# The two running maxima of a graph attention kernel move from PSUM to SBUF

## Chip, cores, metric

One core of one Trainium2 chip. The metric is the time of one launch on the device in microseconds (us); lower is better.

## The reference, cut to what matters

```python
h = jnp.maximum(_layernorm(x), 0.0)                # x: 3125 nodes x 128
x = x + gat(relu(gat(h, W1 ...)), W2 ...)          # two layers, 103125 edges (src, dst)
h = jnp.maximum(_layernorm(x), 0.0)
x = x + gat(h, W ...)                              # third layer

def gat(x, src, dst, W, a_src, a_dst, b):
    h = x @ W
    e = leaky_relu((h @ a_src)[src] + (h @ a_dst)[dst], 0.2)
    m = segment_max(e, dst)
    ex = exp(e - m[dst])
    z = segment_sum(ex, dst)
    return segment_sum((ex / z[dst])[:, None] * h[src], dst) + b
```

The attention is a softmax over the edges that end in a node. For it the kernel needs, for each destination node, the greatest source term among its neighbours.

## The kernel before

The 3125 nodes are 25 tiles (T) of 125 (P). The kernel does not walk the edges in the layers. It first builds a matrix C of edge counts, source by destination, held whole in SBUF as 8-bit floats: 125 partitions (sources within a tile) by 5 chunks (NC) by 25 source tiles by 625 destinations (CD). A count is stored as half of itself.

**Count stage** (to about 204 us). VectorE (DVE) compares keys with an iota (`one_hots`, line 951), 40 steps (NT); TensorE multiplies the one-hot matrices (`count`, line 1780) and signals `half_ok`; ScalarE writes the result into C (line 1452) and signals `half_out`. The one-hots lie in `scratch`, in two buffers by the parity of the step. The first chunk of the first layer is already multiplied by POOL and TensorE in this stage, but not its maxima.

**Layers.** 15 chunks (Q = 3 layers x 5), each 625 destinations by 25 source tiles `s`. For each tile:
- a product block of 125 x 625 in a ring of `slot`s: either DVE makes it (`product`, line 1149: maximum of the row term in PSUM and a scalar, times C), or ScalarE does the maximum in two passes (lines 1567 and 1569) and POOL (GpSimd) multiplies by C (line 751). In a chunk of the last layer POOL has 15 of the 25 tiles; it also scales and adds the chunk before (lines 756, 767, 776, 779).
- TensorE multiplies the block with the features (`products`, line 1813, and `last_products`, line 1821), into PSUM banks 0 and 1.

**The running maxima.** Beside that DVE finds the greatest source term of each destination, chunk by chunk. `top_step` (lines 1051 to 1069) takes the minimum of the counts and a scalar of the source tile (0 where there is no edge, the scaled term where there is) and the maximum with what is there: one instruction of 625 elements for each of the 25 tiles. There are two running maxima, for even and for odd tiles (`in_odd`), so that two instructions that follow each other do not wait for each other's result; the first of each is a tensor_scalar (line 1069), the others scalar_tensor_tensor (line 1067). The last odd one is written to `top_a`, in SBUF, and `join_tops` (line 1073) joins the even maximum into it. TensorE transposes `top_a` (line 1789), DVE reduces it (line 1079), and from that come the factors `back`, `kappa` (ScalarE, line 1550) and `rz` for the softmax of the chunk. The maxima of a chunk run while the products of the same chunk run, 5 of them (AHEAD) at the end of the chunk before; in the first layer they are spread by `FIRST_TOPS`, since none was made in the count stage.

**Where things lie.** In the usual path both running maxima lie in PSUM at columns TOP0 and TOP1. `side` and `side_c` are two blocks of 625 columns of `scratch` in SBUF, at columns 4405 and 5030, which only the careful path (a branch that these inputs do not take) used; they lie over the one-hot buffer of the odd steps (columns 4096 to 8191).

**Order.** Every engine runs its list in the order written. Before the first maximum DVE makes the last one-hots (step 39, an odd one, lines 1248 and 1249) and waits for `half_out[1]` (line 1250), that is for the ScalarE copy of step 38. `set_mode`, `extremes_early`, `negative_r` (line 1040) and others are small instructions on DVE between the large ones; line 880 is one of the start.

Of the kernel before, what the change touches and what calls it, by code (L numbers as in the profile page):

```python
# [7 lines left out]
def gat_stack_kernel(nc, x, edges, apart, W1, a_src1, a_dst1, b1, W2, a_src2, a_dst2, b2,  # L8
# [3 lines left out]
    ALU, ACT, AX = mybir.AluOpType, mybir.ActivationFunctionType, mybir.AxisListType  # L12
# [6 lines left out]
    P = 125  # L19
# [16 lines left out]
    CD = CT * P  # L36
# [17 lines left out]
    NT = NC * JT  # L54
# [12 lines left out]
    with ctx:  # L67
# [3 lines left out]
        def sem(name):  # L71
            return ctx.enter_context(nc.semaphore(name))
# [113 lines left out]
        top_a = scratch[0:P, at:at + CD]  # L186
# [13 lines left out]
        side = scratch[0:P, at:at + CD]  # L200
        side_c = scratch[0:P, at + CD:at + 2 * CD]
# [4 lines left out]
        ps = ctx.enter_context(nc.psum_tensor("ps", [128, 8 * 512], fp32))  # L206
# [12 lines left out]
        ROWU, TOP1, TOP0, WORK, NEW = 1024, 1664, 2304, 3072, 3072  # L219
# [58 lines left out]
        half_ok = [sem("half0_ok"), sem("half1_ok")]  # L278
# [164 lines left out]
        def in_odd(k, q=None):  # L443
            if q in (1, 2):
                return k % 2 == 1 and not any(at_ == AFTER and (c, k) == (q, k_) for at_, c, k_ in FIRST_TOPS[q])
            return k >= AHEAD and k % 2 == 1
# [423 lines left out]
        def _(dve):  # L870
            v = nc.vector
# [68 lines left out]
            def one_hots(t, part=None):  # L940
                c, i = t // JT, t % 2
                first, last_w = SPLIT[t % JT], SPLIT[t % JT + 1]
                w0, w1_ = 0, last_w - first
                if part is not None:
                    w0, w1_ = HALF[part][0], min(HALF[part][1], w1_)
                if t > 1 and w0 == 0:
                    dve.wait_ge(half_ok[1], t - 1)
                for n, (hot, key, m) in enumerate(((hot_lo[i], key_lo, COLS), (hot_col[i], key_col, P))):
                    if t % JT == 0:
                        dve.wait_ge(keys_sb, 2 * c + n + 1)  # L950
                    last = v.tensor_tensor(hot[:, w0:w1_, :, :],  # L951
                                           key[:, c, first + w0:first + w1_, :].unsqueeze(2).broadcast_to(
                                               [128, w1_ - w0, m, LANES]),
                                           iota_ps[:, 0:m, :].unsqueeze(1).broadcast_to([128, w1_ - w0, m, LANES]),
                                           ALU.is_equal)
                last.then_inc(hots_ok, 1)
# [94 lines left out]
            def top_step(S, unit, q, s):  # L1051

                counts = C5[:, q % NC, s, :]
                n = q * (T + 1)
                odd = in_odd(s, q if S is F else None)
                at_ = TOP1 if odd else TOP0
                top = ps[0:P, at_:at_ + CD]
                same = [k for k in range(s) if in_odd(k, q if S is F else None) == odd]
                if same:
                    dve.wait_ge(S.top_done, n + same[-1] + 1)  # L1060
                elif q:
                    dve.wait_ge(S.top_done, n)
                if s == LAST_ODD and q:
                    dve.wait_ge(S.top_T, q)
                dest = top_a if s == LAST_ODD else top
                if same:
                    v.scalar_tensor_tensor(dest, counts, unit[:, s:s + 1], top, ALU.min, ALU.max).then_inc(S.top_done, 1)  # L1067
                else:
                    v.tensor_scalar(dest, counts, unit[:, s:s + 1], None, ALU.min).then_inc(S.top_done, 1)  # L1069

            def join_tops(S, q):
                dve.wait_ge(S.top_done, q * (T + 1) + T)
                v.tensor_tensor(top_a, top_a, ps[0:P, TOP0:TOP0 + CD], ALU.max).then_inc(S.top_done, 1)

            def maxima(S, q, part, scale, low):
                tc = slice(q % NC * CT, (q % NC + 1) * CT)
# [76 lines left out]
            def next_top(q, k):  # L1153
                L = q // NC
                if turn(q) and k in (0, EARLY_TILES, LATE):
                    dve.wait_ge(unit_ready, 3 * L - 1 + (0, EARLY_TILES, LATE).index(k))
                top_step(F, a_unit[L % 2], q, k)

            def first_tops(q, s):
                for at_, c, k in FIRST_TOPS[q]:  # L1160
                    if at_ == s:
                        next_top(c, k)
                        if k == T - 1:
                            join_tops(F, c)

            def chunk(q):
                L, c = q // NC, q % NC
                for s in range(T):
# [4 lines left out]
                    if q < len(FIRST_TOPS):  # L1173
                        first_tops(q, s)
                    else:
                        for k in range(AHEAD, T):
                            if top_at(q, k) == s:
                                next_top(q, k)
                        if s == join_at(q):
                            join_tops(F, q)  # L1180
# [67 lines left out]
            one_hots(NT - 1, 0)  # L1248
            one_hots(NT - 1, 1)
            dve.wait_ge(half_out[1], NT)  # L1250
            dve.wait_ge(unit_ready, 1)
            for k in range(AHEAD):
                next_top(0, k)
# [113 lines left out]
            def careful_chunk(q):  # L1367
                L, c = q // NC, q % NC
                b = ab[L][:, c * CT:(c + 1) * CT, 1]
                for i in range(T):  # L1370
                    top_step(K, a_unit[0], q, i)
                join_tops(K, q)
                for part in range(3):
                    maxima(K, q, part, span[:, 1:2], b_low[0])
                if q:
                    dve.wait_ge(K.rows_ready, q)
                dve.wait_ge(K.m_lin, 2 * q + 2)
                v.tensor_tensor(uv[:, 0, :], b, m_top[:, :], ALU.subtract)
                v.scalar_tensor_tensor(uv[:, 1, :], b, SLOPE, m_top[:, :], ALU.mult, ALU.subtract).then_inc(uv_ready, 1)
                for s in range(T):  # L1380
                    A, B, n = slot[s], side, q * T + s
                    dve.wait_ge(e_ready, n + 1)
                    v.tensor_tensor(B, A, B, ALU.max).then_inc(mx_done, 1)
                    dve.wait_ge(mx_done, n + 1)
                    v.scalar_tensor_tensor(A, B, 2.0, C5[:, c, s, :], ALU.min, ALU.mult).then_inc(p_ready, 1)
                    if c:
                        careful_after(q - 1, s)
                    if s == LEAD - 1:
                        rest_steps(q)
# [308 lines left out]
        def _(pe):  # L1698
# [71 lines left out]
            def count(t, by_halves=False):  # L1770
                i, n = t % 2, SPLIT[t % JT + 1] - SPLIT[t % JT]
                for j, (w0, w1_, _) in enumerate(HALF):
                    at_ = place(t, j)
                    if j == 0 or by_halves:
                        pe.wait_ge(hots_ok, t + 1 + j)
                    pe.wait_ge(half_out[j], t + 1)
                    for w in range(w0, min(w1_, n)):
                        o = at_ + 128 * (w - w0)
                        for k in range(KC):
                            last = mm(ps[0:128, o:o + WC], hot_lo[i][:, w, :, k], hot_col[i][:, w, :, k],  # L1780
                                      start=(k == 0), stop=(k == KC - 1))
                    last.then_inc(half_ok[j], 1)
# [260 lines left out]
```

## Time and profile before

| what | us |
|---|---|
| median of 3 runs | 687.71 (687.67 to 689.26) |
| the profiled execution | 687.7 |
| its span, first to last instruction | 686.0 |
| busy in the span: DVE | 639.8 (93%) |
| PE (TensorE) | 587.9 (86%) |
| ACT (ScalarE) | 484.7 (71%) |
| POOL (GpSimd) | 459.6 (67%) |

The profiled execution lies at the median of the runs. The profile is of this one execution. Start times count from the start of the span. PEld is TensorE's weight load beside the matmuls. A group of instructions is named by its line, engine, operation and "out<-in" by the program's names; `ps` is the PSUM tensor, `C`, `scratch`, `gathered`, `hB` and the rest lie in SBUF.

### The profile page before, as it was taken

What the parts mean: (1) busy time and instruction counts of PE and PEld (TensorE: products, weight loads), DVE (VectorE), ACT (ScalarE), POOL (GpSimd) and SP (SyncE); (2) the same over time, 40 slices, a digit from 0 to 9 for tenths busy, and PEclk for the clock granted to TensorE, in tenths of its full rate; (3) what the DMA queues carried; (4) which work ended last, traced back from release to release, by engine and by line L of the source; (5) the groups of instructions that cost most, each with busy time, mean ns of one, the idle gap of its engine ahead of it and who ended that gap; (6) DMA issues with size and microseconds to landing.
All of it is one profiled execution on the core that took longest, in us unless ns stands there. A gap on an engine that the chain in (4) does not pass through costs nothing.

```text
span 686.0 us, 13824 instructions
## 1 busy us (share of the span) xinstructions
PE 587.9 (86%) x5571; PEld 570.1 (83%) x5571; DVE 639.8 (93%) x911; ACT 484.7 (71%) x719; POOL 459.6 (67%) x448
## 2 busy tenths in 40 slices
PE   1728845989869899999999979999989989999995
PEld 1628744988769899989999979899989979999994
DVE  3999979999999989999987999999998899999994
ACT  0416543655969787887765878989886698898891
POOL 5579103589908656675954775858598688697883
PEclk9959977899999899999999999999999999999998
DMA  2410002000000000000100100000010010110001
GB/s 69 119 56 2 1 9 38 1 2 1 20 1 1 20 1 20 1 1 9 20 20 1 27 1 20 1 19 2 8 20 20 1 27 3 37 29 11 20 1 42
DMA packets 22325, 12.07 MB, mean 18 GB/s; under 512 B 12393, under 2 KB 20055, under 8 KB 22255
## 3 DMA queue, kind: packets, MB, share of 16 engines
q1 hardware_dynamic: 21455, 9.85, 6.2%
q0 software_dynamic: 800, 1.26, 0.6%
q8 instruction: 46, 0.75, 0.5%
q14 instruction: 24, 0.20, 0.1%
HBM read 9.47 MB, written 1.64 MB: 16 GB/s over the span
## 4 chain that ended last, share of the span: by engine, by line
DVE 52%; PE 28%; issue 8%; DMA 6%; POOL 4%; ACT 1%; POOLq 0%; DVEq 0%; SPq 0%
PE ps L1813 21%; DVE scratch L951 21%; DVE ps L1067 16%; DVE scratch L1149 5%; DMA xr<-in_x 3%; POOL scratch L751 2%; DVE ps L1069 2%; DVE ps L1079 1%; PE ps L1866 1%; PE ps L1821 1%; DMA gathered<-ext_lines 1%; PE ps L1844 1%; DVE scratch L1067 1%; DMA gathered<-in_edges,start_i 1%; DMA ext_lines<-ext 1%
## 5 line engine op out<-in xcount | busy, mean ns | idle before, releaser
L1813 PE MATMUL ps<-hB,scratch 125*125 125x129 f32 x3450 | 404.7, 276 | 21.3 <-DVE scratch L1149 17.8
L1813 PEld LDWEIGHTS ps<-hB,scratch 125*125 125x125 f32 x3450 | 390.7, 189 | 28.6 <-DVE scratch L1149 23.0
L751 POOL TENSOR_TENSOR scratch<-scratch,C 125x625 f32<-125x625 f32 x239 | 304.1, 1283 | 124.1 <-ACT scratch L1569 122.1
L1067 DVE SCALAR_TENSOR_TENSOR ps<-C,a_unit,ps 125x625 f32<-125x625 fp8e3 x330 | 275.5, 867 | 2.3
L1567 ACT ACTIVATE scratch<-gathered,r_neg 125x625 f32<-125x625 f32 x219 | 176.6, 806 | 18.7 <-PE ps L1813 17.5
L1569 ACT ACTIVATE scratch<-scratch,r_src 125x625 f32<-125x625 f32 x219 | 179.0, 817 | 7.1
L1452 ACT ACTIVATE C<-ps 125x1000 fp8e3<-125x1000 f32 x80 | 78.0, 1000 | 78.5 <-PE ps L1780 78.3
L1780 PE MATMUL ps<-scratch 128*128 128x125 bf16 x1250 | 90.3, 235 | 40.0 <-DVE scratch L951 38.1
L1780 PEld LDWEIGHTS ps<-scratch 128*128 128x128 bf16 x1250 | 83.0, 105 | 46.8 <-DVE scratch L951 44.7
L1149 DVE SCALAR_TENSOR_TENSOR scratch<-ps,r_src,C 125x625 f32<-125x625 f32 x121 | 104.2, 861 | 4.2 <-PE ps L1803 4.1
L951 DVE TENSOR_TENSOR scratch<-key_lo,ps 128x4096 bf16<-128x4096 bf16 (+3 forms) x41 | 89.8, 2190 | 0.0
L951 DVE TENSOR_TENSOR scratch<-key_col,ps 128x4000 bf16<-128x4000 bf16 (+3 forms) x41 | 87.9, 2144 | 0.0
L1069 DVE TENSOR_SCALAR ps<-C,a_unit 125x625 f32<-125x625 fp8e3 x30 | 25.8, 865 | 0.2
L756 POOL TENSOR_TENSOR scratch<-scratch,rz 125x640 f32<-125x640 f32 x14 | 17.6, 1258 | 11.8 <-DVE rz L1126 11.8
L743 POOL TENSOR_SCALAR scratch<-gathered,r_src 125x625 f32<-125x625 f32 x20 | 15.7, 783 | 10.7 <-DMA gathered<-g_lines 10.7
L1550 ACT ACTIVATE kappa<-back 125x5 f32<-125x5 f32 x15 | 3.1, 207 | 27.0 <-DVE back L1093 26.9
L1821 PE MATMUL ps<-hB,scratch 125*125 125x129 f32 x150 | 21.6, 274 | 0.0
L1821 PE MATMUL ps<-hB,gathered 125*125 125x129 f32 x150 | 21.4, 273 | 0.0
L728 POOL TENSOR_TENSOR shift<-sigma,tau 125x1 f32<-125x1 f32 x3 | 0.6, 192 | 30.7 <-DVE tau L1013 30.7
L1079 DVE TENSOR_REDUCE ps<-ps 125x5 f32<-125x625 f32 x15 | 12.2, 812 | 8.2 <-PE ps L1789 8.2
L790 POOL TENSOR_TENSOR hB<-hA,e_src 125x645 f32<-125x645 f32 x15 | 19.0, 1265 | 0.0
L1821 PEld LDWEIGHTS ps<-hB,scratch 125*125 125x125 f32 x150 | 18.8, 187 | 0.2 <-POOL scratch L751 0.2
(195 smaller groups left out, 451.5 us busy)
## 6 DMA issues: line engine op xcount, KB each, us to landing
gathered<-g_lines SPq DMA_DIRECT2D x15, 305.2 KB
xr<-in_x SPq DMA_DIRECT2D x1, 1562.5 KB
out<-xr SPq DMA_DIRECT2D x4, 312.5 KB
edge_sb<-in_edges SPq DMA_DIRECT2D x1, 805.7 KB
gathered<-ext_lines SPq DMA_DIRECT2D x5, 122.1 KB
w<-in_W SPq DMA_DIRECT2D x2, 128.0 KB
out<-xr SPq DMA_DIRECT2D x1, 187.5 KB
out<-xr SPq DMA_DIRECT2D x1, 125.0 KB
```

The lines of the kernel that those rows point to most:

```text
L751: g.tensor_tensor(slot[s], slot[s], C5[:, q % NC, s, :], ALU.mult).then_inc(pool_done, 1)
L951: last = v.tensor_tensor(hot[:, w0:w1_, :, :], key[:, c, first + w0:first + w1_, :].unsqueeze(2).broadcast_to([128, w1_ - w0, m, LANES]), ...
L1067: v.scalar_tensor_tensor(dest, counts, unit[:, s:s + 1], top, ALU.min, ALU.max).then_inc(S.top_done, 1)
L1069: v.tensor_scalar(dest, counts, unit[:, s:s + 1], None, ALU.min).then_inc(S.top_done, 1)
L1079: v.tensor_reduce(mu[:, :], tiles(WORK), AX.X, ALU.max).then_inc(S.top_max, 1)
L1149: v.scalar_tensor_tensor(slot[s].rearrange("p (t n) -> p t n", n=P), tiles(ROWU), r_src[L % 2][:, s:s + 1], C5[:, c, s, :].rearrange("p (t ...
L1452: a_.activation(C5[:, c, :, rows].rearrange("p t (w q) -> p t w q", q=WQ), tiles(place(t, i), w1_ - w0).rearrange("p w (t q) -> p t w q", ...
L1567: a_.activation(A, ga[q % 2], ACT.Relu, bias=r_neg[L % 2][:, s:s + 1]).then_inc(over_done, 1)
L1569: a_.activation(A, A, ACT.Identity, bias=r_src[L % 2][:, s:s + 1]).then_inc(rowmax_ok, 1)
L1780: last = mm(ps[0:128, o:o + WC], hot_lo[i][:, w, :, k], hot_col[i][:, w, :, k], start=(k == 0), stop=(k == KC - 1))
L1813: last = mm(ps[0:P, acc_at(t):acc_at(t) + HW], A[:, P * t:P * (t + 1)], feat, start=opens and t in (0, 3), stop=closes, skip_group_check=True)
L1821: last = mm(ps[0:P, acc_at(t):acc_at(t) + HW], slot[s][:, P * t:P * (t + 1)], hB3[:, s, :], start=False, stop=s == T - 1, skip_group_check ...
```

## The change

Both running maxima of the usual path take the two blocks `side` and `side_c` of `scratch`, in SBUF, in place of the two in PSUM; `top_a` stays where it was. All maxima and the join read and write there. Since the blocks lie over the odd one-hot buffer, DVE also waits, before the first maximum, until TensorE has multiplied the last step (`half_ok[1]`). `top_step` and `join_tops` are shared with the careful path, whose maxima move too.

```diff
@@ top_step
                 odd = in_odd(s, q if S is F else None)
-                at_ = TOP1 if odd else TOP0
-                top = ps[0:P, at_:at_ + CD]
+                top = side if odd else side_c
@@ join_tops
-                v.tensor_tensor(top_a, top_a, ps[0:P, TOP0:TOP0 + CD], ALU.max).then_inc(S.top_done, 1)
+                v.tensor_tensor(top_a, top_a, side_c, ALU.max).then_inc(S.top_done, 1)
@@ before the first maximum
             dve.wait_ge(half_out[1], NT)
+            dve.wait_ge(half_ok[1], NT)
             dve.wait_ge(unit_ready, 1)
```

## Rows read from the trace of the kernel before

**Rows 1.** Stretches: busy time (instructions) of each engine, granted PE clock, DMA.

```profile
core 0: us, PE busy (x) PEld busy (x) DVE busy (x) ACT busy (x) POOL busy (x), PEclk, DMA share, GB/s
0.00:203.29 203.29, 137.25 (x1616) 128.03 (x1616) 187.29 (x168) 102.00 (x138) 115.56 (x122) 0.91 0.11 27
203.29:671.00 467.71, 444.12 (x3902) 436.04 (x3903) 447.62 (x726) 381.73 (x579) 340.27 (x324) 0.99 0.05 13
671.00:686.00 15.00, 6.51 (x56) 6.04 (x54) 4.88 (x19) 0.97 (x3) 3.77 (x3) 0.88 0.17 45
```

**Rows 2.** Stretches: one chunk of the last layer.

```profile
203.29:224.20 20.91, 18.51 (x165) 17.87 (x165) 20.71 (x27) 20.37 (x27) 15.53 (x16) 1.00 0.01 2
594.82:623.98 29.16, 28.97 (x260) 28.77 (x260) 28.95 (x45) 25.67 (x36) 23.87 (x20) 1.00 0.08 23
```

**Rows 3.** Page, part 4: the chain that ended last, by engine.

```profile
DVE 52%; PE 28%; issue 8%; DMA 6%; POOL 4%; ACT 1%; POOLq 0%; DVEq 0%; SPq 0%
```

**Rows 4.** Groups on DVE: busy us, mean ns, idle before.

```profile
L1067 DVE SCALAR_TENSOR_TENSOR ps<-C,a_unit,ps 125x625 f32<-125x625 fp8e3 x330 | 275.5, 867 | 2.3
L1149 DVE SCALAR_TENSOR_TENSOR scratch<-ps,r_src,C 125x625 f32<-125x625 f32 x121 | 104.2, 861 | 4.2 <-PE ps L1803 4.1
...
L1069 DVE TENSOR_SCALAR ps<-C,a_unit 125x625 f32<-125x625 fp8e3 x30 | 25.8, 865 | 0.2
L1067 DVE SCALAR_TENSOR_TENSOR scratch<-C,a_unit,ps 125x625 f32<-125x625 fp8e3 x15 | 12.9, 859 | 0.0
...
L1073 DVE TENSOR_TENSOR scratch<-scratch,ps 125x625 f32<-125x625 f32 x15 | 12.1, 808 | 0.5
```

**Rows 5.** Groups on POOL, 203 to 671 us: the products.

```profile
L751 POOL TENSOR_TENSOR scratch<-scratch,C 125x625 f32<-125x625 f32 x207 | 262.8, 1281 | 113.0 <-ACT scratch L1569 112.6
```

**Rows 6.** Timeline: start us, duration us, what. POOL and DVE together.

```profile
605.71 3.68 POOL L751 TENSOR_TENSOR scratch<-scratch,C 125x625 f32<-125x625 f32 x3
...
606.24 3.19 DVE L1067 SCALAR_TENSOR_TENSOR ps<-C,a_unit,ps 125x625 f32<-125x625 fp8e3 x4
```

**Rows 7.** Timeline at 393 us.

```profile
393.44 1.25 POOL L751 TENSOR_TENSOR scratch<-scratch,C 125x625 f32<-125x625 f32 x1 [0.31 <-ACT scratch L1569]
393.49 1.20 DVE L1020 SCALAR_TENSOR_TENSOR counts_fit<-ext_all,covers 1x1 f32<-1x1 f32 x1
```

**Rows 8.** Groups on DVE: small instructions.

```profile
L1086 DVE SCALAR_TENSOR_TENSOR ps<-ps,e_top 125x5 f32<-125x5 f32 x15 | 2.5, 165 | 0.0
...
L1113 DVE TENSOR_TENSOR ps<-scratch,kappa x14: 152/166/170, 229.5 to 657.2; 125x5 f32<-125x5 f32 x14
```

**Rows 9.** Timeline at 359 us.

```profile
359.44 1.26 POOL L756 TENSOR_TENSOR scratch<-scratch,rz 125x640 f32<-125x640 f32 x1
360.00 0.73 DVE L1040 TENSOR_SCALAR r_neg<-r_src 125x5 f32<-125x5 f32 x1
```

**Rows 10.** Timeline at 3 us.

```profile
3.11 1.53 POOL L636 IOTA hB<- 128x256 bf16 x1
3.27 1.71 DVE L880 TENSOR_SCALAR scratch<-hA,sampled 125x625 f32<-125x625 f32 x1 [0.52 <-POOL numbers L634]
```

**Rows 11.** Timeline at 15 us.

```profile
14.54 1.21 POOL L641 DMA_INDIRECT gathered<-in_edges,start_i  x1 [0.30 <-issue]
...
16.02 0.28 DVE L913 TENSOR_SCALAR hB<-hB 125x256 f32<-125x256 f32 x1
16.05 1.33 POOL L641 DMA_INDIRECT gathered<-in_edges,start_i  x1 [0.30 <-issue]
```

**Rows 12.** Groups on DVE: two inputs in SBUF, in the tail.

```profile
L1244 DVE SCALAR_TENSOR_TENSOR xr<-scratch,rz,xr 125x128 f32<-125x128 f32 x5 | 1.5, 348 | 0.1
```

**Rows 13.** Timeline of POOL at 591 us; in brackets the idle time before.

```profile
591.65 1.25 POOL L751 TENSOR_TENSOR scratch<-scratch,C 125x625 f32<-125x625 f32 x1 [2.68 <-ACT scratch L1569]
```

**Rows 14.** Timeline at the end of the count stage.

```profile
203.29 0.90 DVE L1069 TENSOR_SCALAR ps<-C,a_unit 125x625 f32<-125x625 fp8e3 x1
...
203.47 0.76 PE L1780 MATMUL ps<-scratch 128*128 128x125 bf16 x10 [0.33 <-DVE scratch L951]
```

**Rows 15.** Stretches of the count stage.

```profile
86.00:103.00 17.00, 8.29 (x98) 7.53 (x96) 13.54 (x18) 7.99 (x15) 1.25 (x5) 0.80 0.05 9
137.00:154.00 17.00, 14.73 (x186) 14.00 (x184) 17.00 (x9) 9.39 (x12) 13.85 (x13) 1.00 0.01 2
```

## Prediction

> **What bounds the kernel now.** I read the stretches first. Until 203.29 us the kernel counts edges and no running maximum exists; from there to 671.00 the attention layers run, and the last 15.00 us are the tail [rows 1]. Only the middle stretch, 467.71 us, holds instructions that the change touches. In it VectorE (DVE) is busy 447.62 us, TensorE 444.12, ScalarE 381.73 and GpSimd (POOL) 340.27: two engines are at 95%, ScalarE is at 82% and POOL at 73%. One chunk of the last layer (29.16 us) shows the same more sharply: PE 28.97, DVE 28.95, POOL 23.87, ACT 25.67 [rows 2]. The chain that ended last puts 52% on DVE and 28% on PE [rows 3]. So time that DVE loses between two products goes nearly whole into the end, and POOL can lose about 5 us a chunk before it sets the pace itself.
>
> Then the groups. The running maxima of the usual path are 330 scalar_tensor_tensor of 867 ns, which read the counts in SBUF and the maximum in PSUM, and 30 tensor_scalar of 865; 15 more of the first kind write top_a, and 15 joins take 808 [rows 4]. That is 390 instructions, 26 a chunk. DVE's other large work, the products (121 into scratch, 10 into the last slot), reads its rows from PSUM and stays as it is. POOL's work is 207 products of 1281 ns in that stretch, each reading two tensors in SBUF [rows 5]. Last, what the two engines do at once: four maxima follow each other in 3.19 us, so (3.19 - 0.86)/3 = 0.777 us from start to start, while POOL has three products of its own in 3.68 us, 1.21 apart [rows 6]. Neither feels the other. Today no running maximum takes two tensors from SBUF.
>
> **What the change does.** It removes and adds no instruction but one wait. All 360 maxima and joins get two SBUF inputs, and the 30 tensor_scalar have SBUF on both sides. The question is what such an instruction costs beside a busy POOL, and the trace has it in small samples:
> - At 393.49 a scalar_tensor_tensor of one element, both tensors in SBUF, took 1.20 us and ended at 394.69; a POOL product ran from 393.44 to 394.69 [rows 7]. Its kind, with one input in PSUM, takes 165 ns [rows 8]. So it waited about 1.04 us, until some 0.16 before the recorded end of POOL's instruction.
> - At 360.00 a tensor_scalar of 5 elements, SBUF to SBUF, took 0.73 and ended at 360.73; POOL's instruction ended at 360.70 [rows 9].
> - At 3.27 a tensor_scalar of 625 elements took 1.71 and ended at 4.98; a POOL iota ended at 4.64 [rows 10]. It ran within 0.34 + 0.16 = 0.50 us once let in.
> - Against it: the 14 small products with kappa have two SBUF inputs too and took 152 to 170 ns [rows 8]. Each started where POOL had no large instruction under way, since they stand behind the exponential for which ScalarE and then POOL wait; so they don't contradict it.
>
> I read: such a DVE instruction is let in only when the POOL instruction under way is through. The Trainium skill ("SBUF — State Buffer", section "Who interferes with whom") says that a DVE instruction with two SBUF inputs contends with a GpSimd instruction that reads SBUF, that a 2-port mode does too, and that whichever starts first keeps the shared pair for the whole instruction. By that rule the sum is the serial one below; the trace agrees for DVE waiting on POOL (1.20 us for one element).
>
> The other direction, POOL waiting for DVE, has one weak sample: the POOL instruction at 16.05, beside a DVE tensor_scalar from SBUF to SBUF at 16.02, took 1.33 where the one before took 1.21 [rows 11]. I take it as mutual.
>
> **The sum.** If the two exclude each other, the stretch must hold all of POOL's instructions and all 390 maxima one after the other; products of DVE (131) and its small work still lie beside POOL.
> - Upper end: POOL 340.3 us as it is, maxima 390 x 0.777 = 303.0. Together 643.3.
> - Lower end: POOL lets go 0.16 us early in each of its 324 instructions [rows 1], 340.3 - 51.8 = 288.5. DVE holds only while it streams: from 128 elements in 348 ns [rows 12] and 625 in 861 [rows 4], (861 - 348) / 497 = 1.032 ns an element and 216 ns fixed, so it streams 0.645 us; 360 x 0.645 = 232.2. The tensor_scalar's 0.50 less the same 0.22 is 0.28, 30 x 0.28 = 8.4. Together 529.1.
> - I take the middle, 586: handing over hides something of each instruction's fixed part, but not all in an engine that issues in order.
> - Idle port: once a chunk POOL has nothing ready for about 2.7 us (a wait for ScalarE at 591.65) [rows 13]. 14 x 2.7 = 37 us. At most maxima fill it (nothing added); I keep it, since the products of DVE come late now and free the buffers late. Stretch: 623 us.
>
> The added wait: DVE's first maximum starts at 203.29, and the last count matmuls, whose buffers the new place overlaps, end at 203.47 + 0.76 = 204.23 [rows 14]. Queued behind it are all maxima and products of chunk 1; DVE is 20.7 of 20.9 us busy there, so I take the whole 0.9 us; the lower bound is 0, if chunk 1 is paced by the port anyway.
>
> Sum against the profiled execution (span 686.0, run 687.7, so 1.7 outside; it equals the median of 687.71): 203.3 + 0.9 + 623 + 15.0 + 1.7 = 844 us. Ends of the same case: 529 + 37 gives 787, 643 + 37 gives 901. One chunk as a cross-check: 23.9 + 26 x 0.777 = 44.1, at the lower end 20 x (1.21 - 0.16) + 24 x 0.645 + 2 x 0.28 = 37.0, middle 40.6 and 2.7 idle, 43 us in place of 29.2.
>
> What is late next: POOL's products reach PE later, so PE, now waiting 0.2 us in such a chunk, falls to 444 of 623 us busy (71%).
>
> **The rivals.**
> *Only DVE waits.* POOL starts its next instruction although a DVE maximum is reading. Then a maximum beside a busy POOL costs 1.21 in place of 0.777, 0.43 more, for each POOL product that meets one: 207 x 0.43 = 89 us at most, 67 if a quarter fall on products instead. Stretch 535 to 557, end 756 to 778, say 770. For it: a sample for mutual exclusion hardly exists. Against: the instruction at 16.05 took 0.12 longer beside DVE, and POOL often waits for ScalarE between its products (113.0 us in all) [rows 5], so it is not always ready with the next one.
>
> *The clock falls.* With TensorE at 71%, its granted clock may drop to the lower level at times. From 137 to 154 us PE was busy 14.7 of 17 us at a granted clock of 1.00; from 86 to 103 it was busy 8.3 of 17 at 0.80, that is partly at 1.2 GHz in place of 2.4 [rows 15]. 71% lies between. At 0.80 the 444 us become 555: they fit into 623, but the chunks in which the fall hits stretch; half of the 111 us give 900 and more, up to 950 with the upper end of the sum.
>
> *Faster.* The samples above are special and the large forms stream past POOL. Then what stays is a cheaper maximum: a tensor_scalar from SBUF to SBUF needed 0.50 us when let in [rows 10] instead of 0.865, so 30 x 0.37 = 11 us of DVE. For the two-input forms I have drawn one line through 348 ns (both inputs in SBUF) and 861 (one in PSUM) [rows 4, 12]; were the true slope 1.0 ns an element, the fixed parts would be 220 and 236 ns, and at 0.95 it would be 226 and 267, so SBUF could save 0 to 40 ns, at most 14 us over 360. DVE is 52% of the chain: half of 11 to 25 us, 0.9 for the wait given back, 676 to 683 us. This rival holds if POOL's instructions release the port element by element rather than whole; the one-element instruction that took 1.20 us speaks against it. The Trainium skill ("VectorE: DVE Perf Modes", section "The TRN2 errata — SBUF-src ops pay a fixed extra latency per instruction") gives 58 cycles fixed from SBUF and 120 from PSUM. By its figures each of the 390 would save 62 cycles, 65 ns, an estimate of 25 us in all and about 676 us with half of it in the chain; no run so far shows it.
>
> *Nothing changes:* maxima fall into POOL's gaps. POOL is busy 340 of 468 us, so its gaps of 128 us cannot hold 303 us of maxima.
>
> **How the numbers follow.** Mutual exclusion 0.72, 844 (787 to 901). Only DVE waits 0.11, 770. Clock or the upper end passed 0.08, 900 to 950. Faster 0.06, 680. Same 0.03. About 0.3% is what a measurement can tell here. The range must hold 8 in 10: the first case with the greater part of the second, 765 to 905. Faster 0.06, same 0.03, slower 0.91.
>
> **What the profile after would show.** Right: maxima of 625 elements that take up to 1.9 us, their ends 0.5 to 0.7 us behind the end of a POOL product; POOL products with means well above 1281 ns, or spaced by 1.7 to 2.0 us; DVE's busy time up by far more than its instruction count; products from PSUM still at 861 ns; PE waiting for POOL and DVE in every chunk. POOL products still at 1.28 us and 1.21 apart beside long maxima: only DVE waits. A granted clock below 0.95 in the stretch: the second rival. Wrong altogether: maxima at 800 to 870 ns beside a busy POOL. The forecast fails in size first of all by the hold of one maximum and by how often the port lies idle.

## The result and the profile after

The changed kernel takes 852.04 us (median of 5 runs, 848.06 to 852.68), the kernel before 687.71; the ratio is 1.2367 (95% interval 1.2332 to 1.2401). The profiled execution of after is one of its shorter ones: 848.1 us, span 846.3. So it stands 160 us above the profiled execution before, and the median 164 us above the median.

The page's busy times, then the stretches (us, then busy time and instructions of PE, PEld, DVE, ACT, POOL, the granted clock, DMA): the layers and the tail, and one chunk of the last layer.

```profile
PE 641.7 (76%) x5571; PEld 614.7 (73%) x5571; DVE 803.2 (95%) x911; ACT 488.4 (58%) x719; POOL 588.2 (69%) x448
...
core 0: us, PE busy (x) PEld busy (x) DVE busy (x) ACT busy (x) POOL busy (x), PEclk, DMA share, GB/s
203.20:831.30 628.10, 495.93 (x3920) 478.73 (x3920) 608.30 (x724) 385.38 (x579) 468.84 (x324) 0.92 0.04 10
831.30:846.30 15.00, 4.62 (x38) 4.04 (x36) 7.57 (x21) 0.97 (x3) 3.81 (x3) 0.81 0.11 31
...
790.10:832.20 42.10, 33.55 (x257) 32.00 (x256) 41.85 (x46) 22.66 (x31) 34.13 (x20) 0.92 0.04 9
```

The layers take 628.1 us in place of 467.7, the tail the same 15.0 [rows 1]. ScalarE's busy time has hardly moved (385 and 382). DVE's has grown by 161 us and POOL's by 129, though neither has an instruction more. The chunk takes 42.1 in place of 29.2 us [rows 2], and DVE still counts as busy in 41.9 of them.

The groups (busy us, mean ns of one, idle before) say in which instructions the time lies:

```profile
L1066 DVE SCALAR_TENSOR_TENSOR scratch<-C,a_unit,scratch 125x625 f32<-125x625 fp8e3 x345 | 435.4, 1292 | 2.3
L1148 DVE SCALAR_TENSOR_TENSOR scratch<-ps,r_src,C 125x625 f32<-125x625 f32 x121 | 103.7, 857 | 4.5 <-PE ps L1803 4.5
...
L1068 DVE TENSOR_SCALAR scratch<-C,a_unit 125x625 f32<-125x625 fp8e3 x30 | 27.6, 924 | 1.1 <-issue 0.9
L1072 DVE TENSOR_TENSOR scratch<-scratch 125x625 f32<-125x625 f32 x15 | 22.9, 1526 | 0.5
...
L751 POOL TENSOR_TENSOR scratch<-scratch,C 125x625 f32<-125x625 f32 x239 | 386.2, 1632 | 142.3 <-ACT scratch L1569 140.3
L756 POOL TENSOR_TENSOR scratch<-scratch,rz 125x640 f32<-125x640 f32 x14 | 24.9, 1777 | 24.3 <-DVE rz L1125 24.3
...
L805 POOL TENSOR_TENSOR xr<-xr,b2r 125x128 f32<-125x128 f32 x25 | 21.3, 858 | 0.0
```

The 345 maxima took 867 ns in PSUM [rows 4] and take 1292 now, the joins 1526 in place of 808. DVE's product, which reads PSUM, is where it was (857 and 861). POOL's products went from 1.28 to 1.63 us over the whole run [rows 5 has those of the layers], although their own operands did not move. The excess on DVE is 345 x 0.426 + 15 x 0.718 + 30 x 0.059 = 147.0 + 10.8 + 1.8 = 159.6 us: all of the 160 by which the profiled execution is longer. Counted record by record, 227 of the 390 took over 0.95 us. Of the other 163 the two-input ones took about what they took before; the short tensor_scalars are looked at below.

One such meeting, in the timeline of DVE and of POOL:

```profile
807.27 1.83 DVE L1066 SCALAR_TENSOR_TENSOR scratch<-C,a_unit,scratch 125x625 f32<-125x625 fp8e3 x1
...
806.55 1.88 POOL L751 TENSOR_TENSOR scratch<-scratch,C 125x625 f32<-125x625 f32 x1 [1.32 <-ACT scratch L1569]
```

POOL's product ends at 806.55 + 1.88 = 808.43, the maximum at 809.10, 0.67 later. Over all two-input instructions among these 227 the end lies 0.665 to 0.670 us behind a POOL end (10th to 90th percentile, from the records). A maximum of 0.85 us is thus let in some 0.18 us before the recorded end of POOL's instruction, an estimate from the two lengths. The other direction is in the records too: 167 of POOL's 244 products took over 1.4 us, and the end of such a one lies 1.10 to 1.17 us behind the end of a maximum.

The tensor_scalar that begins each running maximum has only one input in SBUF, but its output is there as well. It waits in the same way:

```profile
575.36 1.61 DVE L1068 TENSOR_SCALAR scratch<-C,a_unit 125x625 f32<-125x625 fp8e3 x1
...
575.33 1.30 POOL L751 TENSOR_TENSOR scratch<-scratch,C 125x625 f32<-125x625 f32 x1 [4.62 <-ACT scratch L1569]
```

Its end is 0.34 us behind POOL's, and 21 of the 30 end 0.34 to 0.35 us behind one. Without a wait it takes about 0.54 us, so its mean of 924 ns hides both a gain and a wait.

And where both have work without a break:

```profile
820.62 0.86 DVE L1148 SCALAR_TENSOR_TENSOR scratch<-ps,r_src,C 125x625 f32<-125x625 f32 x1
821.40 6.84 DVE L1066 SCALAR_TENSOR_TENSOR scratch<-C,a_unit,scratch 125x625 f32<-125x625 fp8e3 x4
...
820.00 5.51 POOL L751 TENSOR_TENSOR scratch<-scratch,C 125x625 f32<-125x625 f32 x3
825.47 2.11 POOL L779 TENSOR_TENSOR xr<-xr,b3r 125x640 f32<-125x640 f32 x1
827.54 1.86 POOL L751 TENSOR_TENSOR scratch<-scratch,C 125x625 f32<-125x625 f32 x1
```

POOL starts a product at 820.00 and, three later, the next instruction at 825.47: 1.82 apart, and 1.82 again to 829.36. Before it was 1.21 [rows 6]. One maximum of DVE goes between two of POOL's. They take turns.

PE waited for DVE's products and for POOL's, and POOL for ScalarE (us in total, times, longest). The last line is from the kernel before:

```profile
POOL scratch L751 <- ACT scratch L1569: 140.3, 58, 17.6
...
PE ps L1813 <- DVE scratch L1148: 90.7, 56, 5.0
...
PE ps L1813 <- POOL scratch L751: 19.1, 12, 3.6
...
PE ps L1813 <- DVE scratch L1149: 17.8, 24, 3.6
```

### The profile page after: what moved, and what is told of

It is laid out like the page before. It is cut to its first block, busy times and chain, and to the rows that moved or that the text cites. A ratio compares the mean times of both kernels' runs of the same rounds, so it can differ in the third digit from the quotient of the medians.

```text
span 846.3 us, 13824 instructions
## 1 busy us (share of the span) xinstructions
PE 641.7 (76%) x5571; PEld 614.7 (73%) x5571; DVE 803.2 (95%) x911; ACT 488.4 (58%) x719; POOL 588.2 (69%) x448
## 4 chain that ended last, share of the span: by engine, by line
DVE 49%; issue 15%; POOL 6%; PE 5%; ACT 0%; POOLq 0%; DVEq 0%
DVE scratch L1066 34%; DVE scratch L1148 6%; PE ps L1813 4%; POOL scratch L751 3%; DVE scratch L1068 2%; DVE ps L1078 1%; DVE gathered L1148 1%; PE ps L1789 1%; DVE scratch L1072 1%; DVE bn6c L1132 0%; DVE scratch L951 0%; POOL hB L790 0%; POOL scratch L756 0%; POOLq L67 0%; DVE ps L1085 0%
## 5 line engine op out<-in xcount | busy, mean ns | idle before, releaser
L1813 PE MATMUL ps<-hB,scratch 125*125 125x129 f32 x3450 | 444.9, 290 | 110.0 <-DVE scratch L1148 90.7
L1813 PEld LDWEIGHTS ps<-hB,scratch 125*125 125x125 f32 x3450 | 424.7, 201 | 124.9 <-DVE scratch L1148 102.5
L751 POOL TENSOR_TENSOR scratch<-scratch,C 125x625 f32<-125x625 f32 x239 | 386.2, 1632 | 142.3 <-ACT scratch L1569 140.3
L1066 DVE SCALAR_TENSOR_TENSOR scratch<-C,a_unit,scratch 125x625 f32<-125x625 fp8e3 x345 | 435.4, 1292 | 2.3
L756 POOL TENSOR_TENSOR scratch<-scratch,rz 125x640 f32<-125x640 f32 x14 | 24.9, 1777 | 24.3 <-DVE rz L1125 24.3
L1068 DVE TENSOR_SCALAR scratch<-C,a_unit 125x625 f32<-125x625 fp8e3 x30 | 27.6, 924 | 1.1 <-issue 0.9
L1542 ACT ACTIVATE scratch<-ps 125x387 f32<-125x387 f32 x15 | 7.3, 490 | 34.3 <-PE ps L1821 34.3
L1821 PE MATMUL ps<-hB,scratch 125*125 125x129 f32 x150 | 23.1, 287 | 1.1 <-POOL scratch L751 0.6
L1072 DVE TENSOR_TENSOR scratch<-scratch 125x625 f32<-125x625 f32 x15 | 22.9, 1526 | 0.5
L790 POOL TENSOR_TENSOR hB<-hA,e_src 125x645 f32<-125x645 f32 x15 | 23.3, 1550 | 0.0
L1789 PE MATMUL ps<-ident,scratch 125*125 125x125 f32 x75 | 14.1, 332 | 12.0 <-DVE scratch L1072 11.3
```

Source lines behind the costliest of these rows:

```text
L751: g.tensor_tensor(slot[s], slot[s], C5[:, q % NC, s, :], ALU.mult).then_inc(pool_done, 1)
L1072: v.tensor_tensor(top_a, top_a, side_c, ALU.max).then_inc(S.top_done, 1)
L1813: last = mm(ps[0:P, acc_at(t):acc_at(t) + HW], A[:, P * t:P * (t + 1)], feat, start=opens and t in (0, 3), stop=closes, skip_group_check=True)
L1821: last = mm(ps[0:P, acc_at(t):acc_at(t) + HW], slot[s][:, P * t:P * (t + 1)], hB3[:, s, :], start=False, stop=s == T - 1, skip_group_check ...
```

## Experiments

### Which operand does it: reading or writing

The maximum can be put half in each memory. In the first kernel each reads the old maximum from PSUM and writes to SBUF; in the second it reads it from SBUF and writes to PSUM. The wait of the change is in both. The first edit is against the kernel before, the second against the kernel after; lines without a sign stand in both. The running maximum isn't carried on in either, so their attention is shifted by other values than the reference's.

```diff
 # reads PSUM, writes SBUF (against the kernel before)
                 top = ps[0:P, at_:at_ + CD]
+                to = side if odd else side_c
...
-                dest = top_a if s == LAST_ODD else top
+                dest = top_a if s == LAST_ODD else to if same else top
...
             dve.wait_ge(half_out[1], NT)
+            dve.wait_ge(half_ok[1], NT)
 # reads SBUF, writes PSUM (against the kernel after)
                 top = side if odd else side_c
+                at_ = TOP1 if odd else TOP0
+                to = ps[0:P, at_:at_ + CD]
...
-                dest = top_a if s == LAST_ODD else top
+                dest = top_a if s == LAST_ODD else to if same else top
```

> The 345 scalar_tensor_tensor read the counts from SBUF and the running maximum from PSUM, as before, but write to SBUF, as after. (The maximum is then not carried on: each takes the first of its set in place of the last. The first of each set and the join are as before.) If the second SBUF input is the cause: as before, 688 us (683 to 693), each 0.87 us, POOL products 1.28 us. If writing to SBUF, or SBUF as a place, is the cause: near 852 us.

Measured: 690.11 us, ratio 1.0021 (1.0012 to 1.0030). Maxima and POOL products (groups):

```profile
L1068 DVE SCALAR_TENSOR_TENSOR scratch<-C,a_unit,ps 125x625 f32<-125x625 fp8e3 x345 | 284.9, 857 | 2.4 <-POOL a_unit L718 0.2
...
L751 POOL TENSOR_TENSOR scratch<-scratch,C 125x625 f32<-125x625 f32 x239 | 304.7, 1288 | 124.7 <-ACT scratch L1571 122.6
```

> The 345 scalar_tensor_tensor read counts and running maximum from SBUF, as after, but write to PSUM, as before. (The maximum is not carried on; the first of each set goes to SBUF as after.) If the second SBUF input is the cause: as after, 852 us (842 to 858), means of 1.25 to 1.3 us, POOL products at about 1.8 us beside them. If it is the write: near 688 us.

Measured: 852.58 us, ratio 1.2375 (1.2356 to 1.2394).

```profile
L1068 DVE SCALAR_TENSOR_TENSOR ps<-C,a_unit,scratch 125x625 f32<-125x625 fp8e3 x330 | 421.9, 1308 | 2.3
...
L751 POOL TENSOR_TENSOR scratch<-scratch,C 125x625 f32<-125x625 f32 x239 | 387.0, 1636 | 144.3 <-ACT scratch L1571 142.0
```

For the scalar_tensor_tensor the write is free (690.1 is also what the added wait alone gives, below). The whole slowdown comes back with the second input in SBUF and the result in PSUM. It is the read, and it takes POOL's products along: 1288 ns without, 1636 with it. The two kernels say nothing of the 30 tensor_scalars, which write to PSUM in the first and to SBUF in the second.

### Is it POOL, or SBUF as a place

POOL's large instructions in the layers are cut to 5 columns, in the kernel after and in the kernel before. This leaves out most products, the scaling, the residual and the bias sums; every wait and signal stays. Of the edit only the product is shown, the others are of the same kind.

```diff
-                g.tensor_tensor(slot[s], slot[s], C5[:, q % NC, s, :], ALU.mult).then_inc(pool_done, 1)
+                n_ = CD if q == 0 else CT
+                g.tensor_tensor(slot[s][:, 0:n_], slot[s][:, 0:n_], C5[:, q % NC, s, 0:n_], ALU.mult).then_inc(pool_done, 1)
```

> The kernel after, with POOL's large instructions of the layer stretch cut to 5 columns (products, scaling, residual, biases; so most of that arithmetic is left out), all waits and signals kept. DVE's own work is untouched. Exclusion theory: with POOL's instructions at 0.2 us in place of 1.3 the maxima wait for next to nothing; a few us below the same cut of the kernel before, since the 30 tensor_scalar to SBUF save 0.3 us each: 672 to 692 us, maxima at 0.84 to 0.9 us. If SBUF is dearer by itself: over 50 us above that cut of the kernel before.

> The kernel before with the same cut of POOL's instructions. POOL had 5 us a chunk to spare in the last layer, so little changes: 675 to 688 us. It is the reference for the kernel after with the same cut: the difference of the two is what the place alone costs or gives, without POOL. Exclusion theory: within 10 us of each other, after not slower by more than 5.

Measured: 682.79 us after (ratio to the kernel before 0.9927, 0.9905 to 0.9950) and 683.01 before (0.9919, 0.9900 to 0.9938), so the 164 us between the two kernels are gone. First the groups of the cut kernel after, then of the cut kernel before:

```profile
L1068 DVE SCALAR_TENSOR_TENSOR scratch<-C,a_unit,scratch 125x625 f32<-125x625 fp8e3 x345 | 286.6, 862 | 2.3
...
L1070 DVE TENSOR_SCALAR scratch<-C,a_unit 125x625 f32<-125x625 fp8e3 x30 | 16.0, 536 | 1.6 <-issue 1.4
L1074 DVE TENSOR_TENSOR scratch<-scratch 125x625 f32<-125x625 f32 x15 | 12.3, 821 | 0.5
...
L752 POOL TENSOR_TENSOR scratch<-scratch,C 125x5 f32<-125x5 f32 x215 | 104.7, 491 | 277.3 <-ACT scratch L1571 277.0
```

```profile
L1069 DVE SCALAR_TENSOR_TENSOR ps<-C,a_unit,ps 125x625 f32<-125x625 fp8e3 x330 | 275.2, 865 | 2.3
...
L1071 DVE TENSOR_SCALAR ps<-C,a_unit 125x625 f32<-125x625 fp8e3 x30 | 25.8, 862 | 0.2
...
L752 POOL TENSOR_TENSOR scratch<-scratch,C 125x5 f32<-125x5 f32 x215 | 41.8, 196 | 362.3 <-ACT scratch L1571 361.0 <-PE ps L1815 1.4
```

Two things are to be read. Without POOL in the way a maximum costs the same from either memory, 862 and 865 ns; only the 30 tensor_scalar gain, 536 in place of 862 ns. And the other direction, which my prediction had from one weak sample, is plain here: POOL's instruction of 5 columns takes 196 ns on average beside maxima in PSUM and 491 beside maxima in SBUF. POOL waits for DVE too. The gain of the tensor_scalar, 30 x 0.33 = 9.8 us of DVE less 0.9 for the wait, doesn't show in the end.

### Half of the maxima

```diff
-                top = side if odd else side_c
+                top = ps[0:P, TOP1:TOP1 + CD] if odd else side_c
```

> Only the even running maximum lies in SBUF, the odd one is back in PSUM. Of the 26 instructions of a chunk 16 then have two inputs in SBUF (14 scalar_tensor_tensor, the join) or SBUF on both sides (one tensor_scalar), 10 have one input in PSUM. Exclusion theory: the port no longer sets the pace (POOL 288 to 340 us and 240 x 0.645 to 0.777 = 155 to 186 us are 443 to 526 us, against 448 us of DVE's own work), what is left are single waits of DVE; 240 instructions, 7 in 10 meeting a POOL instruction with half a microsecond to go, give 84 us: 740 to 780 us. If SBUF is dearer for each instruction by itself, the extra 164 us are shared by count: 16/26 of them, 789 us. Odd maxima stay at 0.87 us with both.

Measured: 788.79 us, ratio 1.146 (1.1442 to 1.1477). My 740 to 780 was too low, and the figure of the theory that a maximum in SBUF is dearer by itself, 789, was met. That theory is refuted by the kernels with short POOL instructions above (862 and 865 ns), so the meeting is by its count and not by its cause. The groups, and the border of two chunks in the timeline:

```profile
L1066 DVE SCALAR_TENSOR_TENSOR scratch<-C,a_unit,scratch 125x625 f32<-125x625 fp8e3 x210 | 263.3, 1254 | 2.3
...
L1066 DVE SCALAR_TENSOR_TENSOR ps<-C,a_unit,ps 125x625 f32<-125x625 fp8e3 x120 | 103.2, 860 | 0.0
...
L1072 DVE TENSOR_TENSOR scratch<-scratch 125x625 f32<-125x625 f32 x15 | 26.0, 1733 | 0.5
...
692.59 7.28 DVE L1066 SCALAR_TENSOR_TENSOR scratch<-C,a_unit,scratch 125x625 f32<-125x625 fp8e3 x4
...
701.47 2.51 PE L1813 MATMUL ps<-hB,scratch 125*125 125x129 f32 x10 [5.27 <-DVE scratch L1148]
...
705.76 1.31 POOL L751 TENSOR_TENSOR scratch<-scratch,C 125x625 f32<-125x625 f32 x1 [4.74 <-ACT scratch L1569]
```

The odd maxima in PSUM stay at 860 ns. Those in SBUF take 1254, little less than with all of them there (1292). I had taken them as single meetings spread evenly. They are not: at the end of a chunk the join, a tensor_scalar and 4 even maxima follow one another, each of the two-input ones taking 1.74 to 1.80 us, while POOL works off what is ready. DVE's next product is late by as much; PE waits 5.27 us for it, frees no buffer, and POOL then stands 4.74 us without work. The excess is 210 x 0.388 + 15 x 0.925 + 15 x 0.08 = 96.6 us by the groups, and the span is 785.4 - 686.0 = 99.4 us longer. The waits of DVE again account for nearly everything.

### Less work for POOL

Two tiles more in each of 8 chunks go to DVE, whose product reads PSUM.

```diff
-        MORE = (0, 6, 12, 18, 22)
+        MORE = (0, 12, 22)
```

> The kernel after, with 2 more tiles in each of 8 chunks (second and third layer, not the first chunk of a layer) made by DVE in place of ScalarE and POOL: 16 products from PSUM more on DVE, 16 products less on POOL. If the shared port sets the pace: each tile frees 1.0 to 1.1 us of it, and the product of DVE, which does not need it, runs beside POOL's next instruction: 16 x 1.0 = 16 us less, 836 us; at the least 16 x 0.2 = 3 us less, where the wait that goes (1.77 - 0.78) only just outweighs the product (0.78). If DVE is the bound and its waits are no matter: 16 x 0.78 = 12 us more, 864 us.

Measured: 842.83 us, ratio 1.2245 (1.2220 to 1.2269): 9 us faster than the changed kernel, between the 3 and the 16 us that I had given for a shared port.

```profile
L1066 DVE SCALAR_TENSOR_TENSOR scratch<-C,a_unit,scratch 125x625 f32<-125x625 fp8e3 x345 | 419.9, 1244 | 2.3
L1148 DVE SCALAR_TENSOR_TENSOR scratch<-ps,r_src,C 125x625 f32<-125x625 f32 x137 | 117.2, 856 | 0.0
...
L1072 DVE TENSOR_TENSOR scratch<-scratch 125x625 f32<-125x625 f32 x15 | 23.2, 1543 | 0.5
...
L751 POOL TENSOR_TENSOR scratch<-scratch,C 125x625 f32<-125x625 f32 x223 | 358.5, 1623 | 163.2 <-ACT scratch L1569 161.2
```

DVE does 16 products more, 16 x 0.78 = 12.5 us, and its maxima wait less: 345 x (1.292 - 1.244) = 16.6 us. Net 4 us on DVE, with spans of 846.3 and 841.2 (the profiled execution of the changed kernel is one of the shorter ones, so the medians are further apart). So an engine that is 95% "busy" got more work and the kernel got faster, since part of its busy time was waiting for POOL. That the port (the way into SBUF for which both engines wait) is what counts is supported; that it is full is not, a full one would have given all 16.

### Does the clock of TensorE cost anything

The granted clock of the layers fell from 0.99 [rows 1] to 0.92, that is, stretches at 1.2 in place of 2.4 GHz. Idle matmuls of zeros behind each tile, into a bank that nothing uses, keep TensorE busier.

```diff
                         products(slot[s], hB3[:, s, :], F.pe_done, s == 0, False, q if s == 0 else 0)
+                        mm(ps[0:P, 2048:2560], zeros[:, 0:P], zeros[:, 0:512], start=True, stop=True,
+                           skip_group_check=True)
```

> The kernel after, with one further matmul of 512 columns on TensorE behind each of the first 23 tiles of a chunk, of zeros, into a PSUM bank that is free: 322 in all, 0.2 us each at the full clock. It keeps TensorE busier while it waits. The granted clock is 0.92 in the layer stretch of after; here it should be over 0.97. If its falls cost time: 5 to 15 us less than 852. If they lie in TensorE's waits: 852 us, or up to 5 us more for the matmuls.

Measured: 854.10 us, ratio 1.2401 (1.2377 to 1.2426). The layers:

```profile
203.20:837.00 633.80, 540.50 (x4257) 511.46 (x4255) 607.42 (x724) 387.59 (x580) 465.71 (x324) 0.95 0.04 10
```

The clock came to 0.95 only, not to the 0.97 that I wanted for the test, so a second kernel takes two such matmuls behind each tile.

> As the kernel with one more matmul behind each tile, with two: 644 matmuls of zeros, 0.2 us each at the full clock, 9 us a chunk; TensorE then works 38 of 42 us in a chunk of the last layer. The one matmul took the granted clock of the layer stretch from 0.92 to 0.95 and the time did not fall. If falls of the clock cost time, this one (0.98 or more) gives 4 to 10 us less than the kernel after beside it. If DVE's waits alone set the pace, the same time within 3 us, or more where the matmuls hold up a real one.

Measured: 856.43 us, ratio 1.2410 (1.2389 to 1.2430).

```profile
203.50:840.00 636.50, 592.00 (x4566) 543.21 (x4564) 606.87 (x724) 388.00 (x580) 462.94 (x324) 0.98 0.04 10
```

> The kernel after, unchanged, on the same chip as the one with two matmuls more, since its five runs lay at 848.1 (granted clock 0.914 to 0.916) and 852.0 to 852.7 (0.904 to 0.906). Clock theory: the same two groups, the faster at the higher clock, and the filled kernel at or below the faster. Otherwise time and clock go apart.

Measured: 852.09 us (848.88 to 854.04), ratio 1.2347 (1.2313 to 1.2381).

```profile
203.50:836.00 632.50, 500.68 (x3927) 482.98 (x3925) 610.41 (x723) 385.52 (x580) 466.35 (x324) 0.91 0.04 10
```

The clock went from 0.91 to 0.95 and 0.98 and the time did not fall; it is 2 to 4 us up. But the idle matmuls have a price of their own. By the three rows the time in which DVE does nothing (stretch less busy time) goes from 22.1 to 26.4 and 29.6 us, and TensorE's share of the chain that ended last goes up. First the kernel after, then the one with two matmuls:

```profile
DVE 64%; issue 16%; PE 8%; POOL 7%; DMA 4%; ACT 1%; POOLq 0%; DVEq 0%; SPq 0%
...
DVE 57%; PE 22%; issue 13%; DMA 4%; POOL 3%; ACT 0%; DVEq 0%; POOLq 0%; SPq 0%
```

So the test excludes that the lower clock costs tens of us, and a gain of a few us from the higher one could be hidden behind the matmuls. In the chain of the unfilled kernel TensorE has 8%, where it had 28% in the kernel before [rows 3]. That fits a clock whose falls lie mostly in time in which TensorE waits, though no run shows where each fall lies.

The changed kernel's own runs come in two groups, and the shorter ones have the higher clock, as the clock theory said: 848 us at 0.914 to 0.916 and 852 at 0.904 to 0.906, in the second set 848.88 at 0.916 and the rest at 0.902 to 0.910. Whether the clock makes these 4 us or only goes with them is open.

### The added wait alone

```diff
             dve.wait_ge(half_out[1], NT)
+            dve.wait_ge(half_ok[1], NT)
```

> The kernel before with only the added wait for the last count step. My sum had 0.9 us for it, with 0 as the lower bound: 688.6 us, ratio 1.0013 (1.000 to 1.002). The first maximum starts at about 204.2 instead of 203.3. If chunk 1 has slack for it, no change.

Measured: 690.13 us, ratio 1.0022 (1.0013 to 1.0031), 1.5 us; 1.3 between the medians. The first maximum (timeline of DVE), here and in the kernel after:

```profile
204.36 0.87 DVE L1069 TENSOR_SCALAR ps<-C,a_unit 125x625 f32<-125x625 fp8e3 x1 [0.91 <-issue]
```

```profile
204.25 0.55 DVE L1068 TENSOR_SCALAR scratch<-C,a_unit 125x625 f32<-125x625 fp8e3 x1 [0.92 <-issue]
```

It starts 1.07 and 0.96 us later than at 203.29 [rows 14], and within the interval all of it arrives at the end. The forecast was 0.9 us.

### The same rule used on the kernel before

The kernel before had a few meetings of its own [rows 7, 9]. One input of each of these small instructions is put in PSUM: a copy of the flag, and a constant -1 to multiply by.

```diff
-                        v.scalar_tensor_tensor(counts_fit[:, :], ext_all[0:1, 0:1], BIG / 10, covers[0:1, :], ALU.is_le,
+                        v.scalar_tensor_tensor(counts_fit[:, :], ext_all[0:1, 0:1], BIG / 10, covers_ps[0:1, :], ALU.is_le,
-                v.tensor_scalar(r_neg[L % 2][:, t0:t1], r_src[L % 2][:, t0:t1], -1.0, None, ALU.mult)
+                v.tensor_tensor(r_neg[L % 2][:, t0:t1], r_src[L % 2][:, t0:t1], minus[:, t0:t1], ALU.mult)
+            v.memset(minus, -1.0)
+            v.tensor_copy(covers_ps, covers[:, :]).then_inc(in_psum, 1)
```

> The kernel before, with its own few meetings at the port taken away, as a try at a better kernel: the one-element instruction that took 1.20 us (line 1020) and the six that negate r_src (0.17 to 0.80 us) get one of their inputs from PSUM (a copy of the flag, and a constant -1), at the cost of one memset and one copy. Together they waited about 1.0 + 0.6 + 0.6 + 0.2 = 2.4 us. Exclusion theory: these become 0.16 to 0.2 us, and 1 to 2.4 us are gained less 0.2 for the two new ones: 685.5 to 687 us, ratio 0.997 to 0.999. If the waits were for something else, they stay as long and the time is the same.

Measured: 686.98 us against 689.84 beside it, ratio 0.9960 (0.9946 to 0.9973): 2.9 us faster, a little more than the 0.997 forecast, and the fastest kernel here that leaves nothing out.

```profile
L1044 DVE TENSOR_TENSOR r_neg<-r_src,ps 125x5 f32<-125x5 f32 x4 | 0.6, 156 | 0.1
...
L1044 DVE TENSOR_TENSOR r_neg<-r_src,ps 125x15 f32<-125x15 f32 x2 | 0.3, 164 | 0.0
...
L1024 DVE SCALAR_TENSOR_TENSOR counts_fit<-ext_all,ps 1x1 f32<-1x1 f32 x1 | 0.1, 143 | 0.0
```

The one-element instruction takes 143 ns where it took 1203 [rows 7], the negations 156 to 164 ns where one took 730 [rows 9]. By the records the seven instructions lost 2.6 us together, and the memset and the copy cost 0.2. Moving one operand the other way, from SBUF to PSUM, is worth 0.4% here.

## Why the prediction came out right

Forecast 844 us with a range of 765 to 905, measured 852. The mechanism was right. That the number is so close is partly luck, since two terms were off in opposite directions (steps 3 and 4). By its steps:

1. *What is there: no meeting of maxima and POOL before, and a one-element instruction of 1.20 us as the key.* Held. The reading "let in about 0.16 us before POOL's recorded end" gives a maximum that ends 0.5 to 0.7 us behind it; it is 0.67. For the tensor_scalar, which I let run 0.50 us from 0.16 before the end, it gives 0.34, and 0.34 it is.
2. *The exclusion is mutual.* Held, though the sample for it was weak. POOL's 5 columns at 491 in place of 196 ns show it. The rule of the Trainium skill that I set beside it ("SBUF — State Buffer", section "Who interferes with whom") says this of two SBUF inputs, and that an instruction with at most one, outside the 2-port modes, does not contend with GpSimd. The runs agree: 690 us with one, 853 with two. That the tensor_scalars with one input in SBUF waited too, once their output was there, shows that the number of inputs is not all of it.
3. *The serial sum, 529 to 643 us, taken at 586.* Counted from the records, a maximum or a POOL instruction runs in 576 of the 628 us of the layers: 10 less than I took. A POOL product and a maximum together take 1.82 us where neither stops; I had 1.05 + 0.645 = 1.70 at the lower end, 1.28 + 0.777 = 2.06 at the upper. But the middle of a range 114 us wide was chosen and not worked out, so that it lay this near is luck in part.
4. *Idle port, 37 us.* Too small. In the other 52 us neither a maximum nor any POOL instruction runs. POOL's waits were longer than my one of 2.7 a chunk, for instance these two of one chunk (timeline of POOL, idle time in brackets):

```profile
799.50 1.30 POOL L751 TENSOR_TENSOR scratch<-scratch,C 125x625 f32<-125x625 f32 x1 [3.09 <-ACT scratch L1569]
...
811.05 1.69 POOL L751 TENSOR_TENSOR scratch<-scratch,C 125x625 f32<-125x625 f32 x1 [2.62 <-ACT scratch L1569]
```

   It is the term that was mis-sized, 15 us short, and the 10 us too many of step 3 made up for most of it. The half experiment shows its nature: bursts of maxima make DVE's product late, PE then frees no buffer, POOL runs dry.
5. *The added wait, 0.9 us.* 1.3 us between medians, with the wait as the only change.
6. *PE at 71%.* Its busy time is 496 of 628, 79%; 444 of 628 would be 71. The granted clock was 0.92 in place of 0.99, which fits the difference; it was not tested by itself.
7. *The rivals.* "Only DVE waits" (770) fell with POOL's own lengthening. The clock did fall, to 0.92, which I had given 8%, but its price of 50 us and more was wrong: DVE's waits account for 160 of the 160 us, and raising the clock to 0.98 brought nothing back. "Faster" fell with the meetings, and of its cheaper maximum only the tensor_scalar came true (536 in place of 862 ns without POOL), which didn't show in the end. For two inputs there is no saving: 862 ns with both in SBUF and POOL out of the way, 857 with one in PSUM and the result in SBUF, 865 with one in PSUM and the result there too. The Trainium skill ("VectorE: DVE Perf Modes", section "The TRN2 errata — SBUF-src ops pay a fixed extra latency per instruction") gives a fixed part of 58 cycles from SBUF and 120 from PSUM, by my estimate from it 65 ns less. The measurement decides against it here.

The sum took the shared port as what sets the pace. The runs say it less strictly: two tiles off POOL gave 9 us and not 16, so the port is not full, and the time is lost in DVE's waits for it. A simpler sum than mine would have been nearer: time before plus DVE's waits. It holds in three kernels (160 of 160 us, 97 of 99, and with two tiles moved 130 + 11 + 3 of waits and 12 of products against 155). I could not have worked it out beforehand without the share of maxima that meet a POOL instruction, which is at least 227 of 390.

## What to carry to other kernels

Before an operand of VectorE moves from PSUM to SBUF, count its inputs: for a scalar_tensor_tensor one in SBUF was free here, and with two it took turns with GpSimd wherever they met, and both engines paid. A tensor_scalar needs a second look: with its one input and its output in SBUF it was shorter by itself, but it waited for GpSimd too. Look in the trace of before for tiny VectorE instructions with two SBUF inputs that end just as a GpSimd instruction ends; one of them gives away the mechanism. And a busy share of 95% can hold waiting; compare the mean time of an instruction, by form, before and after.

## What the runs showed of the hardware

- A VectorE instruction with two SBUF inputs and a GpSimd instruction that reads and writes SBUF exclude each other, whole instruction by whole instruction and in both directions: ends 0.67 us behind POOL's, 1.82 us for a pair of 0.78 and 1.21. Whether GpSimd's reading or its writing does it was not tried.
- A tensor_scalar with its one input and its output in SBUF waits as well (ends 0.34 us behind POOL's), with its output in PSUM it did not (865 ns).
- For the scalar_tensor_tensor the destination does not matter: 690.1 us with one SBUF input and the result in SBUF, 852.6 with two and the result in PSUM.
- Without contention a tensor_scalar of 625 elements from SBUF to SBUF takes 536 ns in place of 862 to PSUM, while scalar_tensor_tensor costs 862 ns from two SBUF inputs and 865 from one.
- TensorE's granted clock fell from 0.99 to 0.92 over the layers, and idle matmuls that raised it to 0.98 brought no time back. DVE stood still 4 to 8 us longer with them, so a price of a few us is not excluded.
